# A routed mixture layer on one core: sums of W on ScalarE, scales and split from chunk 3, the last two pieces inside the dense tile, zeros multiplied at the start

## The chip, the core and the metric

The kernel runs on one core of a Trainium2 chip. A core has TensorE (PE, matrix products into the PSUM banks), VectorE (DVE), ScalarE (ACT), GpSimd (POOL) and SyncE (SP, which here only issues transfers). Each engine works through its own list of instructions in order, and engines wait for one another with semaphores. The metric is the device time of one execution in microseconds; lower is better.

## What is computed

The reference in short (x is 8 sequences of 512 tokens of 256 numbers, in float32):

```python
# first half: an attention of which only the row sums are used
q, k = rope((x @ Wq.T).astype(bf16)), rope((x @ Wk.T).astype(bf16))
o = where(causal, exp(q @ k.T / 16), 0).sum(-1)            # one number a token
x = layernorm(x + relu(o @ fc1_w.T + fc1_b) @ fc2_w.T + fc2_b)
# second half: 12 experts, top 3 of three routers over a = x @ P_w.T
C1, C2, C3 = (softmax over the top 3 of a @ U.T, zero elsewhere, for U in (U1, U2, U3))
h = gelu(sum_e C1[:, e] * (x @ W1[e].T))
y = sum_e C2[:, e] * (h @ W2[e].T) + C3 @ b2
out = layernorm(x + y)
```

## The kernel before, in words

The 4096 tokens are 32 tiles of 128, in eight groups of four. A first stage of eight chunks (`NCH` = 8, four sequences by 128 positions each) computes q and k. Per chunk TensorE makes four projections (`project(c, 0..3)`, four float32 matmuls each), ScalarE copies each out of its bank (`qk_copy`, L497), VectorE rotates queries and keys (`rope(c, 0)` and `rope(c, 1)`), TensorE multiplies them (`scores`), ScalarE takes exponentials with their sums (`exps`), and `gate_transpose` with `gate_relu` bring the sums into place for `fc`. A projection uses one of two banks, and `project` waits until the copy of the projection two before it is done.

W1 and W2, 12 experts each, arrive in float32 and are split into a high and a low float16 part after they were multiplied by a power of two found from their largest magnitude. For W1 VectorE takes that maximum (`w_amax`, three reductions, L977); for W2 ScalarE takes the sum of magnitudes as a bound (`w_sum`, three operations, L514), which VectorE reads in `w_bound` (L985). `peak_transpose` (TensorE), `peak_pow` (VectorE), `peak_spread` (TensorE) and `scales` (VectorE, L999 to L1005, ends in `scale_done`) make the factors of all partitions; `router_split` splits the routers' matrix. Eight of the 12 experts of each W are split by GpSimd, one in each `w_piece` (L377, L379, L380; 16 pieces); the other four of each by ScalarE's `w_high` (L532) with VectorE's `w_low` (L1010), 8 pairs. From chunk 4 on there is one piece at each of the 16 places (c, j), j from 0 to 3, and two pairs per chunk.

Between these lie the steps of groups 0 and 1, placed by hand: `early_aux(c, j, early)` calls step 4(c-3)+j of a list of 18, so they begin at place (3, 0), number 12 of 32, and end at place (7, 1), number 29. On GpSimd they are `norm_scale(0)` at place 15, `norm_scale(1)` at 23, `chosen_exps(0)` (L396) at 28 and `weights_of(0)` (L404 to L407) at 29, each ahead of the piece of its place. VectorE waits for `chosen_exps(0)` in `route_sums(0)` (L1090), which stands at place 29 ahead of both rotations of chunk 7. After the chunks VectorE makes the ids of the chosen experts (`route_ids(0)`, L1080 to L1085).

Then comes the dense tile: tile 0 is multiplied by all 12 experts (`first`, `mixture`, L830; a slot is one expert, six matmuls), while the others use the three experts that their group needs. The slots of the dense tile use two banks in turn, so slot n waits until slot n-2 is taken. ScalarE takes slot 0 (`begin(0)`, which waits for the weights of the routers, `C_done`), VectorE adds the others (`first_mixture`, L1188). In TensorE's order `C3_transpose(0)` (L770), which waits for the ids, stands ahead of the first slot. The last scores, gates and the logits of group 1 lie among the slots. The remaining tiles follow, each with a first mixture, a transpose, a second mixture, and a normalisation.

Of the kernel before, what the change touches and what calls it, by code (L numbers as in the profile page):

```python
# [77 lines left out]
def build(nc, x, xT, wqkT, gate, fc2, p_w, uT, w1T, w2T, b2e, constb, constf, out):  # L78
    ctx = ExitStack()
    with ctx:  # L80
# [85 lines left out]
        RING, HT = 4, 4  # L166
        Z = GT * NR * NE
# [121 lines left out]
        def group(g):  # L289
            return 0 <= g < NG  # L290
# [67 lines left out]
        def _(pool):  # L358
# [81 lines left out]
            for c in range(NCH):  # L440
                for j in range(4):
                    early_aux(c, j, early)
                    if c >= 4:
                        w_piece(piece)
                        piece += 1
# [37 lines left out]
        def _(act):  # L483
# [26 lines left out]
            def w_sum(q):  # L510


                act.wait_ge(ld_w[1], 32)
                act.activation(junk[:, :, :], Wf[:, WS:2 * WS, :][:, PARTS[q], :], ACT.Abs,  # L514
                               accum_out=amaxp[:, 1, q:q + 1]).then_inc(asum_done, 1)
                if q < 2:
                    act.wait_ge(asum_done, q + 1)
# [56 lines left out]
            def aux(k, s, pos):  # L574
                if (s, pos) == (0, 0):
                    if group(k + 1):
                        x1_high(k + 1, 1)
                    if group(k):
                        C3T_copy(k)
                if (s, pos) == (1, 0) and group(k + 1):  # L580
                    exp_route(k + 1)
                if (s, pos) == (2, 0) and group(k + 2):
                    normed(k + 2, 0)
                if (s, pos) == (2, 1) and group(k + 2):
                    normed(k + 2, 1)
                if (s, pos) == (3, 0) and group(k + 2):
                    x1_high(k + 2, 0)
# [16 lines left out]
            act.wait_ge(ld_const, 16 * 6)  # L604
            for c in range(NCH):
                qk_copy(c, 0)
                qk_copy(c, 1)
                if c:
                    exps(c - 1, 0)
                early_aux(c, 0, early)  # L610
                early_aux(c, 1, early)
                if c == 2:
                    w_sum(1)
                if c >= 4:
                    w_high(2 * (c - 4))
                qk_copy(c, 2)
                if c:
                    exps(c - 1, 1)
                qk_copy(c, 3)
                if c:  # L620
                    gate_relu(c - 1)
                early_aux(c, 2, early)
                early_aux(c, 3, early)
                if c in (1, 2):
                    w_sum(2 * (c - 1))
                if c >= 4:
                    w_high(2 * (c - 4) + 1)
# [3 lines left out]
            begin(0)  # L631
            exps(NCH - 1, 0)
            exps(NCH - 1, 1)
# [45 lines left out]
        def _(pe):  # L679
# [32 lines left out]
            def peak_transpose():  # L712
                pe.wait_ge(amax_done, 3)
                pe.transpose(bank[MISC][0:3, 0:P], amax[:, :], identf[:, :]).then_inc(peak_done, 1)
# [83 lines left out]
            def aux(k, s, pos):  # L798
                if (s, pos) == (0, 0) and group(k):
                    C3_transpose(k)  # L800
# [49 lines left out]
            pe.wait_ge(ld_const, 16 * 6)  # L850
            pe.wait_ge(ld_qk, 16)
            for c in range(NCH):
# [3 lines left out]
                if c == 0:  # L856
                    for k in range(NC):
# [3 lines left out]
                if c == 3:  # L861
                    peak_transpose()
                early_aux(c, 1, early)
                if c:
                    scores(c - 1, 0)
                project(c, 2)
                early_aux(c, 2, early)
# [3 lines left out]
                if c == 3:  # L871
                    peak_spread()
# [13 lines left out]
            first(range(0, 4))  # L886
            scores(NCH - 1, 0)
# [59 lines left out]
        def _(dve):  # L947
# [26 lines left out]
            def w_amax(q):  # L974
                if q == 0:
                    dve.wait_ge(ld_w[0], 32)
                r = dve.tensor_reduce(amaxp[:, 0, q:q + 1], Wf[:, 0:WS, :][:, PARTS[q], :], AX.XY, ALU.max,  # L977
                                      apply_absolute_value=True)
                if q == 2:
                    link(r)  # L980
                    dve.tensor_reduce(amax[:, 1:2], amaxp[:, 0, :], AX.X, ALU.max).then_inc(amax_done, 1)

            def w_bound():
                dve.wait_ge(asum_done, 3)
                dve.tensor_reduce(amax[:, 2:3], amaxp[:, 1, :], AX.X, ALU.max).then_inc(amax_done, 1)  # L985
# [169 lines left out]
            for c in range(NCH):  # L1155
                early_aux(c, 0, early)
                early_aux(c, 1, early)
                if c == 4:
                    scales()
                    router_split()  # L1160
# [3 lines left out]
                if c == 1:  # L1164
                    w_amax(0)
                if c == 3:
                    peak_pow()
                early_aux(c, 2, early)
                if c >= 4:
                    w_low(2 * (c - 4))  # L1170
                early_aux(c, 3, early)
                rope(c, 1)
                if c == 1:
                    w_amax(1)
                if c == 2:
                    w_amax(2)
                    w_bound()
                if c >= 4:
                    w_low(2 * (c - 4) + 1)
# [11 lines left out]
            def first_mixture(t):  # L1191
# [5 lines left out]
                for j in range(1, experts_of(t)):  # L1197
# [4 lines left out]
                    add_slot(t, 0, j, sums, sums)  # L1202

# [133 lines left out]
```

## Time and profile before

| | |
|---|---|
| median of 3 runs | 327.04 us (326.6 to 327.73) |
| the profiled execution | 327.78 us, span 325.9 us |
| TensorE busy | 284.7 us (87%) |
| VectorE busy | 256.9 us (79%) |
| ScalarE busy | 155.6 us (48%) |
| GpSimd busy | 115.3 us (35%) |
| mean granted TensorE clock | 0.973 |

In 40 equal slices of the span (8.1 us each), busy tenths of each engine and the granted clock of TensorE in tenths, 9 standing for 90% or more:

```profile
PE   0999999979854988999999899899899997999981
DVE  0069789999976479689889979988988987997672
ACT  1137747655661371435635544634743663634231
POOL 1000018999999102141332431332323314133221
PEclk9999999998995999999999999999999999999997
```

The stage of the chunks is in slices 2 to 12; the dense tile is in slices 13 to 15. GpSimd is busy throughout from slice 7 to slice 13, and slices 12 and 13 are those in which TensorE does least after the start.

### The profile page before, as it was taken

Reading aid. Unit: us, or ns where it says so; the run is one execution under the profiler, and the core shown is the slowest. Engines: PE = TensorE matmul, PEld = TensorE weight load, DVE = VectorE, ACT = ScalarE, POOL = GpSimd, SP = SyncE. Lnnn points to the kernel's source line nnn. Section 1 sums busy time; section 2 is a strip of 40 time slices with the busy share of each in tenths; the row PEclk is TensorE's granted clock in tenths of the full one; section 3 lists DMA queues with packets and bytes.
Section 4 is the critical chain, followed back from the end, with each engine's and each line's share of the span. In section 5 each row is a group of like instructions: output and inputs, shape, how many; then the busy total and the mean of one; then the engine's idle time right before and its main releaser. Section 6 shows DMA issues by size and latency. Waiting matters only on the chain.

```text
span 325.9 us, 6342 instructions
## 1 busy us (share of the span) xinstructions
PE 284.7 (87%) x1978; PEld 191.6 (59%) x1978; DVE 256.9 (79%) x849; ACT 155.6 (48%) x327; POOL 115.3 (35%) x264
## 2 busy tenths in 40 slices
PE   0999999979854988999999899899899997999981
PEld 0444455444323667676677577668577566667771
DVE  0069789999976479689889979988988987997672
ACT  1137747655661371435635544634743663634231
POOL 1000018999999102141332431332323314133221
PEclk9999999998995999999999999999999999999997
DMA  8999999700000000000010000000000010010111
GB/s 230 413 411 218 202 187 186 114 2 0 0 1 0 3 2 0 16 20 18 16 35 16 18 16 27 26 18 19 23 27 19 18 32 19 17 34 19 31 33 37
DMA packets 19235, 20.58 MB, mean 63 GB/s; under 512 B 1600, under 2 KB 18432, under 8 KB 18688
## 3 DMA queue, kind: packets, MB, share of 16 engines
q1 hardware_dynamic: 18480, 19.22, 24.2%
q10 hardware_dynamic: 720, 0.93, 1.0%
q8 instruction: 18, 0.29, 0.4%
q14 instruction: 17, 0.14, 0.1%
HBM read 15.94 MB, written 4.19 MB: 62 GB/s over the span
## 4 chain that ended last, share of the span: by engine, by line
PE 35%; DVE 32%; POOL 16%; issue 7%; ACT 6%; DMA 2%; ACTq 0%; DVEq 0%; POOLq 0%
PE bank L830 20%; DVE early L1188 11%; PE bank L686 9%; POOL W L380 5%; POOL wtmp L377 4%; POOL W L379 3%; DVE st L1225 3%; DVE stats L1036 2%; DVE early L1230 2%; POOL rstd L389 2%; DVE top L1057 2%; DMA gatew<-in_gate 2%; ACT x L546 2%; DVE zrest L1068 2%; PE bank L782 2%
## 5 line engine op out<-in xcount | busy, mean ns | idle before, releaser
L830 PE MATMUL bank<-W,early 128*128 (+1 forms) x630 | 75.6, 273 | 6.3 <-DVE early L1188 4.0
L830 PE MATMUL bank<-W,x1T 128*128 (+1 forms) x630 | 77.3, 278 | 0.5 <-DVE early L1188 0.3
L686 PE MATMUL bank<-early,wqk 128*128 128x512 f32 x128 | 65.1, 642 | 8.6 <-DMA gatew<-in_gate 8.6
L830 PEld LDWEIGHTS bank<-W,x1T 128*128 128x128 f16 x630 | 60.5, 99 | 19.9 <-DVE early L1188 9.5
L830 PEld LDWEIGHTS bank<-W,early 128*128 128x128 f16 x630 | 59.5, 98 | 18.2 <-issue 6.0
L1188 DVE SCALAR_TENSOR_TENSOR early<-bank,Csel,early 128x256 f32<-128x256 f32 x124 | 59.4, 479 | 11.6 <-PE bank L830 7.0
L455 POOL TENSOR_SCALAR ve<-mv 128x1 f32<-128x1 f32 x32 | 7.3, 229 | 120.4 <-DVE mv L1226 120.4
L686 PEld LDWEIGHTS bank<-early,wqk 128*128 128x128 f32 x128 | 23.7, 201 | 30.6 <-issue 21.4
L602 ACT ACTIVATE early<-early 128x256 f32<-128x256 f32 x32 | 13.3, 417 | 50.1 <-DVE early L1188 49.9
L497 ACT ACTIVATE qk<-bank 128x512 bf16<-128x512 f32 x32 | 19.0, 594 | 36.7 <-PE bank L686 36.4
L597 ACT ACTIVATE early<-bank,Csel 128x256 f32<-128x256 f32 x31 | 14.6, 472 | 31.0 <-PE bank L830 30.7
L963 DVE TENSOR_TENSOR xcos<-qk,cb 128x1024 bf16<-128x1024 bf16 x16 | 11.8, 740 | 21.1 <-ACT qk L497 21.0
L388 POOL TENSOR_SCALAR ve<-mv 128x4 f32<-128x4 f32 x8 | 2.3, 283 | 65.9 <-DVE mv L1040 65.8
L645 ACT ACTIVATE early<-bank,ipow 128x256 f16<-128x256 f32 x32 | 15.0, 468 | 17.3 <-PE bank L914 17.3
L380 POOL TENSOR_TENSOR W<-wtmp,W 128x512 f16<-128x512 f32 x16 | 21.0, 1316 | 1.4
L655 ACT ACTIVATE early<-early,shift,rstd 128x256 f32<-128x256 f32 x32 | 18.8, 586 | 5.1 <-POOL shift L457 5.1
L1047 DVE TENSOR_TENSOR x1T<-bank,x1T 128x512 f16<-128x512 f32 x16 | 11.0, 688 | 12.3 <-ACT x1T L553 12.3
L546 ACT ACTIVATE x<-xs,shift,rstd 128x256 f32<-128x256 f32 x32 | 17.4, 591 | 4.3 <-POOL shift L391 4.3
L456 POOL TENSOR_TENSOR rstd<-ve,minus_half 128x1 f32<-128x1 f32 x32 | 18.2, 570 | 2.7
L730 PE MATMUL bank<-fc2s,hgT 32*128 32x256 f32 x64 | 18.0, 400 | 0.0
L782 PE MATMUL bank<-b2s,C3T 64*128 64x512 f32 x32 | 18.0, 641 | 0.0
L507 ACT ACTIVATE expd<-bank 128x128 bf16<-128x128 f32 (+3 forms) x32 | 13.7, 437 | 8.8 <-PE bank L701 8.7
(105 smaller groups left out, 434.0 us busy)
## 6 DMA issues: line engine op xcount, KB each, us to landing
early<-in_xT SPq DMA_DIRECT2D x16, 256.0 KB, 9.4
xs<-in_x SPq DMA_DIRECT2D x32, 128.0 KB, 7.2
out<-early SPq DMA_DIRECT2D x32, 128.0 KB
W<-in_w1T SPq DMA_DIRECT2D x1, 2048.0 KB, 12.1
W<-in_w2T SPq DMA_DIRECT2D x1, 2048.0 KB, 12.3
W<-in_w1T SPq DMA_DIRECT2D x1, 1024.0 KB, 7.7
W<-in_w2T SPq DMA_DIRECT2D x1, 1024.0 KB, 13.8
wqk<-in_wqkT ACTq DMA_DIRECT2D x1, 512.0 KB, 3.9
```

The costliest lines, as they stand in the source:

```text
L380: pool.tensor_tensor(W[:, m, e + 1, 1, :], wtmp[:, n % 2, :], W[:, m, e + 1, 0, :], ALU.subtract)\
L456: link(pool.tensor_tensor(rstd2[:, p:p + 1], ve2[:, p:p + 1], minus_half[:, 0:1], ALU.pow))
L497: act.activation(qk[:, c % 2, g, :, :].rearrange("p s n -> p (s n)"), bank[PROJ[n % 2]][:, :], ACT.Copy)\
L546: n = act.activation(x1[:, g % 3, t, :], xs[:, GT * g + t, :], ACT.Identity, bias=shift[:, g % 2, t:t + 1], scale=rstd[:, g % 2, t:t + 1])
L597: act.activation(acc1[:, t % 2, :], bank[place[n]][:, 0:DIM], ACT.Copy, scale=c0).then_inc(acc_begun, 1)
L645: act.activation(hT[:, t % 2, 0, :, :].rearrange("p c n -> p (c n)"), bank[HT][:, 0:DIM], ACT.Copy, scale=ipow2[:, 1:2]).then_inc(hhi_done, 1)
L655: act.activation(y[:, t % 4, :], y[:, t % 4, :], ACT.Identity, bias=shift2[:, p:p + 1], scale=rstd2[:, p:p + 1]).then_inc(y_done, 1)
L686: mm = pe.matmul(bank[PROJ[n % 2]][:, :], wqk[:, k, g, :], xTb[:, c % 4, k, :, :].rearrange("p s n -> p (s n)"), start=(k == 0), stop=(k = ...
L730: mm = pe.matmul(bank[ROWS][:, t % 2 * DIM:(t % 2 + 1) * DIM], hgT[PAD * T:PAD * (T + 1), u, :, :].rearrange("p b r -> p (b r)"), fc2s[PAD ...
L782: mm = pe.matmul(bank[ROWS][:, :], C3T[rows, :], b2s[rows, :], start=True, stop=True)
L830: mm = pe.matmul(where[:, 0:DIM], lhs(hx, c), w, start=(k == 0), stop=(k == 5))
L1188: dve.scalar_tensor_tensor(sums, bank[place[n]][:, 0:DIM], c, before, ALU.mult, ALU.add)\
```

## The change

Five things are moved or replaced.

1. TensorE multiplies 28 times 128 columns of zeros (read from the cleared C3) by 256 columns of zeros before its first projection, and waits for the constants only after `project(0, 1)`. ScalarE's wait for them is moved behind its first two copies.
2. All six sums of |W| run on ScalarE: W1's in chunk 1, W2's in chunk 2, one in the middle and two at the end of each. VectorE's three maxima are gone, and `w_bound` reads all six.
3. `w_bound` is moved behind `rope(3, 0)`, `peak_transpose` behind `scores(2, 0)`, `peak_spread` behind `project(3, 2)`, and the scales with the routers' split from chunk 4 to chunk 3, ahead of `rope(3, 1)`.
4. GpSimd takes its pieces at places 14 to 29 instead of 16 to 31. Of the eight pairs of `w_high` and `w_low` the first comes at the end of chunk 3, two in each of chunks 4 and 5, one in chunk 6, none in chunk 7: the pairs 6 and 7 are moved into the dense tile, `w_low` behind the adds of slots 2 and 6.
5. `C3_transpose(0)` stands behind slot 3 instead of ahead of slot 0, and `C3T_copy(0)` behind `begin(0)`.

```diff
-                    if c >= 4:
+                    if 14 <= 4 * c + j < 30:
                         w_piece(piece)
...
-            act.wait_ge(ld_const, 16 * 6)
             for c in range(NCH):
                 qk_copy(c, 0)
                 qk_copy(c, 1)
+                if c == 0:
+                    act.wait_ge(ld_const, 16 * 6)
...
-                if c == 2:
-                    w_sum(1)
-                if c >= 4:
-                    w_high(2 * (c - 4))
+                if c in (1, 2):
+                    w_sum(c - 1, 0)
+                if 4 <= c < NCH - 1:
+                    w_high(2 * (c - 4) + 1)
...
                 if c in (1, 2):
-                    w_sum(2 * (c - 1))
-                if c >= 4:
-                    w_high(2 * (c - 4) + 1)
+                    w_sum(c - 1, 1)
+                    w_sum(c - 1, 2)
+                if 3 <= c < NCH - 2:
+                    w_high(2 * (c - 3))
...
             begin(0)
+            C3T_copy(0)
+            w_high(NM * NB - 2)
             exps(NCH - 1, 0)
+            w_high(NM * NB - 1)
...
-            pe.wait_ge(ld_const, 16 * 6)
+            pe.wait_ge(zero_done, 4)
+            zeros = C3[:, :, :].rearrange("p t n -> p (t n)").bitcast(BF16)
+            for n in range(WARM):
+                pe.matmul(bank[SCORE[n % 2]][:, 0:DIM], zeros[:, 0:P], zeros[:, :], start=True, stop=True)
...
-                if c == 3:
-                    peak_transpose()
                 early_aux(c, 1, early)
                 if c:
                     scores(c - 1, 0)
+                if c == 3:
+                    peak_transpose()
                 project(c, 2)
+                if c == 3:
+                    peak_spread()
...
             first(range(0, 4))
+            C3_transpose(0)
             scores(NCH - 1, 0)
...
-            def w_amax(q):
...
-                dve.wait_ge(asum_done, 3)
-                dve.tensor_reduce(amax[:, 2:3], amaxp[:, 1, :], AX.X, ALU.max).then_inc(amax_done, 1)
+                dve.wait_ge(asum_done, 3 * NM)
+                dve.tensor_reduce(amax[:, 1:3], amaxp[:, :, :], AX.X, ALU.max).then_inc(amax_done, 1)
...
-                if c == 4:
-                    scales()
-                    router_split()
                 rope(c, 0)
...
-                if c == 1:
-                    w_amax(0)
                 if c == 3:
+                    w_bound()
                     peak_pow()
                 early_aux(c, 2, early)
-                if c >= 4:
-                    w_low(2 * (c - 4))
+                if 4 <= c < NCH - 1:
+                    w_low(2 * (c - 4) + 1)
                 early_aux(c, 3, early)
+                if c == 3:
+                    scales()
+                    router_split()
                 rope(c, 1)
...
+                if 3 <= c < NCH - 2:
+                    w_low(2 * (c - 3))
...
                     add_slot(t, 0, j, sums, sums)
+                    if t == 0 and j in (2, 6):
+                        w_low(NM * NB - 2 + j // 4)
```

## Rows read from the trace of the kernel before

**Rows 1.** Chain that ended last, start: start us, us, what it was.

```profile
2.87 5.70 DMA gatew<-in_gate
8.61 6.65 PE bank L686 x8
...
25.33 1.77 PE bank L686 x4
```

**Rows 2.** The same chain, from chunk 3 to the dense tile.

```profile
38.05 2.30 DVE amaxp L977
...
50.26 0.18 DVE scale L1005
...
50.53 0.77 POOL wtmp L377
...
91.82 0.42 POOL ez L396
...
102.47 4.77 PE bank L830 x24
```

**Rows 3.** Timeline of TensorE: start us, us, instruction, in brackets idle time before.

```profile
71.81 0.77 PE L753 MATMUL bank<-MT,x1T 128*128 128x36 f16 x24 [1.67 <-DVE x1T L1047]
72.42 3.59 PE L686 MATMUL bank<-early,wqk 128*128 128x512 f32 x4
...
87.70 0.60 PE L699 MATMUL bank<-x1T,qr 128*128 128x512 bf16 x2 [0.99 <-DVE x1T L971]
...
94.18 0.22 PE L762 MATMUL bank<-mask,cb 128*1 128x24 bf16 x3
102.02 0.45 PE L770 MATMUL bank<-identf,C 128*128 128x128 f32 x1 [7.62 <-DVE ids L1085]
...
111.16 3.77 PE L830 MATMUL bank<-W,x1T 128*128 128x256 f16 x30
```

**Rows 4.** Timeline of ScalarE in chunk 2, around a sum of W.

```profile
28.30 1.89 ACT L514 ACTIVATE junk<-W 128x2048 bf16<-128x2048 f32 x1
...
30.31 1.30 ACT L497 ACTIVATE qk<-bank 128x512 bf16<-128x512 f32 x2
```

**Rows 5.** Timeline of VectorE from the wait for GpSimd to its first add.

```profile
92.27 0.30 DVE L1090 TENSOR_REDUCE esum<-ez 128x12 f32<-128x144 f32 x1 [1.33 <-POOL ez L396]
...
102.39 0.67 DVE L1047 TENSOR_TENSOR x1T<-bank,x1T 128x512 f16<-128x512 f32 x1
105.53 0.48 DVE L1188 SCALAR_TENSOR_TENSOR early<-bank,C,early 128x256 f32<-128x256 f32 x1 [2.47 <-PE bank L830]
```

**Rows 6.** Timeline of GpSimd: last clearing, a norm between two pieces, last piece.

```profile
1.38 0.20 POOL L370 MEMSET C<- 128x128 f32 x1
...
73.45 0.55 POOL L388 TENSOR_SCALAR ve<-mv 128x4 f32<-128x4 f32 x1
...
75.82 0.70 POOL L377 TENSOR_SCALAR wtmp<-W,scale 128x512 f32<-128x512 f32 x1
...
103.75 0.70 POOL L377 TENSOR_SCALAR wtmp<-W,scale 128x512 f32<-128x512 f32 x1
...
106.30 0.19 POOL L419 COPY Csel<-C 128x3 f32 x1
```

**Rows 7.** Transfers of chunk 0 (issues from 0.7 to 1.3 us), by tile.

```profile
DMA to landing us min/median/max: 4.6/5.3/5.9
```

**Rows 8.** Groups of instructions by line, VectorE: count, busy us, mean ns of one.

```profile
L1010 DVE SCALAR_TENSOR_TENSOR W<-W,scale 128x512 f16<-128x512 f32 x8 | 8.9, 1107 | 0.2
...
L977 DVE TENSOR_REDUCE amaxp<-W 128x1 f32<-128x2048 f32 x3 | 6.9, 2285 | 0.1
```

**Rows 9.** Timeline of VectorE: rotation, statistics and scales in chunk 3, one multiply later.

```profile
41.18 0.69 DVE L963 TENSOR_TENSOR xcos<-qk,cb 128x1024 bf16<-128x1024 bf16 x1
...
43.30 0.28 DVE L990 TENSOR_REDUCE peak<-bank 3x1 f32<-3x128 f32 x1
...
45.06 1.40 DVE L1036 BATCH_NORM_STATS2 stats<-xs 128x6 f32<-128x256 f32 x4
...
49.54 0.16 DVE L999 COPY pow<-bank 128x3 f32<-128x3 f32 x1
...
77.88 1.64 DVE L964 TENSOR_TENSOR xsin<-qk,cb 128x1024 bf16<-128x1024 bf16 x1
```

**Rows 10.** One stretch by engine: busy us (instructions), granted clock, DMA share, GB/s.

```profile
73.00:74.00 1.00, 1.00 (x2) 0.34 (x1) 0.97 (x2) 0.00 (x0) 0.91 (x2) 0.50 0.00 0
```

More of the change, by code:

```diff
@@ L166, in build @@
         RING, HT = 4, 4
+        WARM = 28
         Z = GT * NR * NE
@@ L508, in exps, with w_sum @@
                                    scale=float(DIM) ** -0.5, accum_out=o[:, c % 2, s:s + 1]).then_inc(exp_done, 1)
[L510 to L517, printed above, removed]
+            def w_sum(m, q):
+                act.wait_ge(ld_w[m], 32)
+                wait(act, asum_done, 3 * m + q)
+                act.activation(junk[:, :, :], Wf[:, WS * m:WS * (m + 1), :][:, PARTS[q], :], ACT.Abs,
+                               accum_out=amaxp[:, m, q:q + 1]).then_inc(asum_done, 1)
             def gate_relu(c):
@@ L577, in aux @@
                         x1_high(k + 1, 1)
-                    if group(k):
+                    if group(k) and k > 0:
                         C3T_copy(k)
@@ L712, in peak_transpose @@
             def peak_transpose():
-                pe.wait_ge(amax_done, 3)
+                pe.wait_ge(amax_done, 2)
                 pe.transpose(bank[MISC][0:3, 0:P], amax[:, :], identf[:, :]).then_inc(peak_done, 1)
@@ L798, in aux @@
             def aux(k, s, pos):
-                if (s, pos) == (0, 0) and group(k):
+                if (s, pos) == (0, 0) and group(k) and k > 0:
                     C3_transpose(k)
@@ L856, in _ @@
                 if c == 0:
+                    pe.wait_ge(ld_const, 16 * 6)
                     for k in range(NC):
@@ L870, in _ @@
                 project(c, 3)
-                if c == 3:
-                    peak_spread()
                 early_aux(c, 3, early)
@@ L972, in rope @@
                 dve.wait_ge(rope_done, 2 * c + part + 1)
-            def w_amax(q):
[L975 to L981, printed above, removed]
             def w_bound():
-                dve.wait_ge(asum_done, 3)
-                dve.tensor_reduce(amax[:, 2:3], amaxp[:, 1, :], AX.X, ALU.max).then_inc(amax_done, 1)
+                dve.wait_ge(asum_done, 3 * NM)
+                dve.tensor_reduce(amax[:, 1:3], amaxp[:, :, :], AX.X, ALU.max).then_inc(amax_done, 1)
             def peak_pow():
@@ L1163, in _ @@
                     router_matrix()
-                if c == 1:
-                    w_amax(0)
                 if c == 3:
+                    w_bound()
                     peak_pow()
                 early_aux(c, 2, early)
-                if c >= 4:
-                    w_low(2 * (c - 4))
+                if 4 <= c < NCH - 1:
+                    w_low(2 * (c - 4) + 1)
                 early_aux(c, 3, early)
+                if c == 3:
+                    scales()
+                    router_split()
                 rope(c, 1)
[L1173 to L1179, printed above, removed]
+                if 3 <= c < NCH - 2:
+                    w_low(2 * (c - 3))
             route_ids(0)
```

## The prediction

> **What bounds the kernel now.** I read the chain of work that ended last first, in order of time, because the change touches only the first 117 us of a span of 325.9 us; what follows is the same code. The chain there has four links. Until 8.61 us TensorE waits for the last constant. Its first eight projection matmuls then take 6.65 us, where later ones take 1.77 us for four: two projections that cost 3.54 us at the full rate cost 3.1 us more [rows 1]. From there TensorE is the bound through chunks 1, 2 and 3, with one hop over VectorE's last maximum of |W| at 38.05. At 50.43 the scales are there, and the chain passes to GpSimd, which splits W piece after piece without a pause until `chosen_exps(0)`, 91.82 to 92.24, the operation that VectorE waits for [rows 2]. The last link is VectorE: sums, two rotations, two `w_low`, the ids at 101.9; TensorE has stood still since 94.4, and the dense tile begins at 102.0, at half rate [rows 2, 3]. ScalarE is not on this chain: its sums of W take 2.0 us each from start to the start of what follows, and nobody waits for them [rows 4].
>
> So the number to follow is when GpSimd reaches `chosen_exps(0)`: VectorE stands 1.33 us in front of its result [rows 5], TensorE waits for VectorE, and no later stage makes up for it.
>
> **The start.** `zero_done` is complete when the memset of C3 ends, at 1.6 us [rows 6]. The 28 products of zeros have 256 columns each. In the dense tile 24 such products took 4.77 us at the half rate, 0.2 us each [rows 2], so 28 take at most 5.7 us and end at 7.4, or sooner if the clock rises among them. Chunk 0 is in 5.9 us after its second issue at 1.3, at 7.2 [rows 7]. I take 7.4 for the first projection, at the full rate: 1.2 us from the earlier start and 3.05 us from the rate, 4.25 us together (4.45 at best; 1.0 if zeros do not lift the clock, which no row shows). Moving the wait for the constants behind `project(0, 1)` costs nothing: they are there at 8.6 [rows 1], and that point is now reached at 10.9. ScalarE's same move is covered likewise, and VectorE's wait for them is as before. The end of `project(1, 3)`, which I call t, moves from 27.10 [rows 1] to 22.85.
>
> **ScalarE's sums.** Six instead of three, and VectorE is rid of three maxima of 2.29 us [rows 8]. But VectorE was not the bound there beyond the one hop, and TensorE can run only two projections ahead of ScalarE's copies, since these have two banks. After `project(1, 3)`: copy and ReLU to t+1.2, two sums to t+5.3, the copy of (2, 0) to t+5.9 [rows 4]. TensorE has done (2, 0), (2, 1) and two scores by t+4.4 and stands for 1.5 us. The sum in the middle of chunk 2 is just covered, and the two at its end reach t+15.4, as `project(3, 1)`, with `fc(0, 0)` before it, ends at t+15.25.
>
> **The order in chunk 3.** `w_bound` now stands behind `rope(3, 0)` on VectorE. That rotation needs the copy of (3, 1), t+16.5, and takes 2.1 us [rows 9]; the bound ends at t+18.8. `peak_transpose` stands on TensorE behind `scores(2, 0)`, which are done at t+15.7. TensorE waits for 3.2 us, with `project(3, 2)`, `fc(0, 1)` and all of chunk 4 queued behind. Then 0.3 us for the transpose, 1.77 for `project(3, 2)` (`peak_pow` is hidden under it), 0.3 for the spread, 1.05 for `fc(0, 1)`: t+22.4. VectorE adds it (0.7) and takes the statistics of group 0 (1.8 us), then come the scales, 0.95 us [rows 9]: t+25.85, against t+23.3 before. On top comes the clock. A stall of 1.67 us before 71.8 was followed by a granted clock of 0.50, and four projection matmuls took 3.59 us instead of 1.77; a stall of 0.99 us before 87.7 was not [rows 3, 10]. 3.2 us is nearly twice the former, so I add 1.8 us once; for the 1.5 us of chunk 2 I take nothing (1.8 more at worst). Scales: 22.85 + 25.85 + 1.8 = 50.5, against 50.43. The whole gain of the start is used up here. The bounds are 46.2 (t+23.3, no stall) and 52.3.
>
> **The queue on GpSimd.** Pieces are taken at places 14 to 29 instead of 16 to 31. `norm_scale(0)` (about 2.2 us) was done before the first piece and now stands behind it; `chosen_exps(0)` stands at place 28, behind 14 pieces instead of 12. Twelve pieces with one `norm_scale` took 50.53 to 91.82, 41.3 us [rows 2]; less 2.4 us for the norm [rows 6] that is 3.24 us a piece. Now 14 x 3.24 = 45.4, 2.2 + 2.4 for two norms, 0.5 for `chosen_exps`, 0.1: 50.5 us from the scales to its end, where it was 41.8. The distance grows by 8.7 us, and the scales come no sooner. A piece beside an idle VectorE took 2.55 us (103.75 to 106.30) [rows 6]; as VectorE will idle before the result, I take off 1.2 us for the last two. `chosen_exps(0)` ends at 50.5 + 50.5 - 1.2 = 99.8, 7.6 us later than at 92.24. Behind that wait are queued on VectorE `route_sums`, both rotations of chunk 7, `route_ids(0)` and the whole dense tile.
>
> **Behind it.** From 92.24 to 103.06, where VectorE was ready for its adds [rows 5], are 10.8 us; two `w_low` leave it, 1.11 us each [rows 8]: 8.65 us. VectorE is ready at 108.45. Before, its first add ran only at 105.53 [rows 5], since TensorE began with `C3_transpose` behind the ids and then at half rate [rows 3]. Now TensorE has slots 0 and 1 done long before, slot 2 as soon as ScalarE begins the tile, and only slot 3 waits for an add: 2.5 us back. From the first add to the end of slot 11 were 105.53 to 114.93, 9.4 us [rows 3, 5]. Into this stretch come two `w_low`, the first behind slot 3, `C3_transpose`, `C3T_copy` and `w_high(6)`. VectorE idles between its adds, which covers half: 10.5 us (9.4 if all is covered; 12.5 if nothing is and slot 3's chain comes on top). Slot 11 ends at 108.45 + 10.5 = 118.95, against 114.93. ScalarE's two `w_high` lie beside VectorE's adds.
>
> **The sum.** Start -4.25, stalls and order in chunks 2 and 3 +2.55, clock +1.8, queue +8.7, its shorter last pieces -1.2, `w_low` out of the tail -2.2, no wait behind the ids -2.5, `w_low` and its waits in the tile +1.1: +4.0. The profiled execution took 327.78 us around its span of 325.9, and this makes it 331.8. The median of the runs lies 0.74 below the profiled one: **331.0 us**, 1.2% slower.
>
> **The rivals.**
> - The clock holds through the stall of 3.2 us: 1.8 us less, 329.2. For it: a stall of 0.99 us did no harm. Against: one of 1.67 us did [rows 3, 10].
> - ScalarE's sums and the new order hold TensorE up nowhere. The scales come at 46.2, and the rest of the sum gives 331.0 - 1.8 - 2.5 = 326.7: no change. For it: three sums so far passed without a stall [rows 4]. Against: two projections ahead is all that two banks allow, and two sums now stand in a row twice.
> - Faster: the pieces shrink. VectorE's second multiply of a rotation takes 1.64 us beside pieces, while the whole rotation took 2.1 before them [rows 9]. If GpSimd is slowed by VectorE as much, a VectorE with less to do lets a piece fall to 2.55 us. It decides from 2.95 us a piece on (4.0 us over 14 pieces). At 2.55 GpSimd would have the result before VectorE comes for it, at about 93: 6.7 us less than 99.8, 324.3. Against: until 91 us VectorE has the same rotations and still six `w_low` to do. The Trainium skill (SBUF — State Buffer, "Who interferes with whom") has it that a VectorE instruction with two SBUF inputs contends with a GpSimd instruction that reads SBUF, and that the one issued second blocks until the first ends. By that rule pieces beside the rotations stay as long as they are; the trace agrees, with 2.55 us beside an idle VectorE and 3.24 us on the mean [rows 2, 6].
> - The zeros don't lift the clock. Only 1.0 us of the start is gained, 3.2 us less: 334.2. The Trainium skill (TensorE: Matmul & The Clock Gate, "What's actually happening") says that the gate goes by how busy the array is, which would count zeros like other data; no row here shows it.
>
> **How the numbers follow.** Forecast 0.50; the clock holds 0.19; no hold-up 0.12; pieces shrink 0.13; zeros in vain 0.06. A measurement of this kernel can tell about 0.3%, 1 us, from no change. So faster 0.13, same 0.12, slower 0.75. The range runs from 326.7, which takes in the case of no change, to 333.5, the forecast with 1.8 us for the clock in chunk 2 and 0.7 for waits in the tile; the fast case and the vain zeros are left out.
>
> **What would show it.** A first projection near 7.4 us at the full rate. A gap of some 3 us on TensorE before the peak transpose and a granted clock of 0.50 behind it. `scale_done` near 50. Fourteen pieces before `ez`, which ends near 100, and VectorE idle for 6 us before it. It is wrong if the scales come at 46 or sooner, or if pieces take less than 3 us on the mean.

## The result and the profile after

The changed kernel takes 331.77 us (median of 4 executions, 330.87 to 332.72), the kernel before 326.82 beside it: a ratio of 1.0151 (95% interval 1.0104 to 1.0198). 331.0 us were forecast. Its profiled execution took 330.93 us with a span of 328.9, 3.15 us above the profiled one of before, where the sum says +4.0.

The slices of the page, 8.2 us each, of TensorE, GpSimd and the granted clock:

```profile
PE   7998697979792998999899999899999997998981
...
POOL 1000019999998002131431432332324223123221
PEclk9999999997996799999999999999999999999998
```

TensorE works from the first slice on now, but slice 13 holds a 2, and GpSimd's block of work ends in the same slice as before, the thirteenth. The chain that ended last (start us, us, what), in the stretch that [rows 1, 2] show of before:

```profile
1.26 5.99 DMA early<-in_xT
...
7.39 3.67 PE bank L691 x8
...
24.11 2.00 ACT junk L516 x2
...
28.72 1.98 PE bank L691 x4
...
41.22 0.17 DVE amax L987
41.43 0.27 PE bank L719
...
47.88 0.18 DVE scale L1007
48.11 0.14 issue
48.24 0.71 POOL wtmp L378
...
51.41 0.57 POOL ve L389
...
97.22 0.43 POOL ez L397
...
106.78 0.40 DVE early L1184
...
114.39 3.61 PE bank L835 x30
```

Read against [rows 1, 2]: the first eight projection matmuls take 3.67 us instead of 6.65 and start 1.2 us sooner. ScalarE's sums (`junk`) have come onto the chain, where none stood. The scales are there at 48.05 instead of 50.43, `chosen_exps(0)` (`ez`) ends at 97.64 instead of 92.24, and slot 11 at 118.0 instead of 114.93. The end of `project(1, 3)` moved from 27.1 to 22.9. So 4.2 us were won by then, 1.8 us of them were lost by the scales, and GpSimd's stretch from the scales to `ez` grew from 41.8 to 49.6 us. The tail behind it, `ez` to slot 11, shrank from 22.7 to 20.4. -2.4 + 7.8 - 2.3 = +3.1 us, the difference of the two executions (3.15 us) to a tenth.

TensorE and VectorE in the changed kernel (start us, us, instruction, in brackets idle time before and what ended it), beside [rows 3, 5]:

```profile
1.63 5.26 PE L859 MATMUL bank<-C 128*128 128x256 bf16 x28 [1.63 <-POOL C L371]
...
28.72 1.98 PE L691 MATMUL bank<-early,wqk 128*128 128x512 f32 x4 [1.56 <-ACT qk L498]
...
41.43 0.27 PE L719 MATMUL bank<-identf,amax 128*3 128x128 f32 x1 [2.94 <-DVE amax L987]
...
103.00 1.46 PE L835 MATMUL bank<-W,x1T 128*128 128x256 f16 x6 [3.62 <-ACT early L597]
107.23 1.46 PE L835 MATMUL bank<-W,x1T 128*128 128x256 f16 x6 [2.77 <-DVE early L1184]
```

```profile
97.67 0.30 DVE L1092 TENSOR_REDUCE esum<-ez 128x12 f32<-128x144 f32 x1 [3.17 <-POOL ez L397]
...
106.71 0.98 DVE L1184 SCALAR_TENSOR_TENSOR early<-bank,C,early 128x256 f32<-128x256 f32 x2
109.86 0.75 DVE L1012 SCALAR_TENSOR_TENSOR W<-W,scale 128x512 f16<-128x512 f32 x1 [2.17 <-ACT W L532]
```

Both stalls of TensorE before the scales are there, 1.56 and 2.94 us. Before the dense tile's third and fourth slot it stands again, for ScalarE and then for VectorE. Both of these had stood for GpSimd: VectorE was idle for 3.17 us in front of `ez`, where it was 1.33 us before [rows 5], and ScalarE began the tile when GpSimd's weights of the routers were there:

```profile
102.47 0.47 ACT L597 ACTIVATE early<-bank,C 128x256 f32<-128x256 f32 x1 [3.48 <-POOL C L408]
```

### The profile page after: what moved, and what is told of

It reads as the page before. It is cut to its first block, busy times and chain, and to the rows that moved or that the text cites. A ratio compares the mean times of both kernels' runs of the same rounds, so it can differ in the third digit from the quotient of the medians.

```text
span 328.9 us, 6402 instructions
## 1 busy us (share of the span) xinstructions
PE 287.4 (87%) x2004; PEld 194.5 (59%) x2006; DVE 249.3 (76%) x845; ACT 161.0 (49%) x333; POOL 114.0 (35%) x264
## 4 chain that ended last, share of the span: by engine, by line
PE 31%; DVE 31%; POOL 18%; issue 8%; ACT 8%; DMA 2%; DVEq 0%; SPq 0%; POOLq 0%; ACTq 0%
PE bank L835 19%; DVE early L1184 11%; PE bank L691 6%; POOL W L381 5%; POOL wtmp L378 4%; POOL W L380 3%; DVE stats L1038 3%; DVE st L1223 3%; DVE early L1228 2%; POOL rstd L390 2%; DMA early<-in_xT 2%; DVE top L1059 2%; ACT x L546 2%; DVE zrest L1070 2%; PE bank L787 2%
## 5 line engine op out<-in xcount | busy, mean ns | idle before, releaser
L691 PE MATMUL bank<-early,wqk 128*128 128x512 f32 x128 | 61.8, 614 | 2.1 <-ACT qk L498 1.6
L691 PEld LDWEIGHTS bank<-early,wqk 128*128 128x128 f32 x128 | 22.8, 194 | 22.9 <-issue 20.1
L378 POOL TENSOR_SCALAR wtmp<-W,scale 128x512 f32<-128x512 f32 x16 | 15.5, 970 | 46.7 <-DVE scale L1007 46.7
L381 POOL TENSOR_TENSOR W<-wtmp,W 128x512 f16<-128x512 f32 x16 | 20.4, 1276 | 1.4
L1184 DVE SCALAR_TENSOR_TENSOR early<-bank,Csel,xs 128x256 f32<-128x256 f32 x31 | 14.8, 478 | 2.6 <-PE bank L835 2.4
## 6 DMA issues: line engine op xcount, KB each, us to landing
W<-in_w2T SPq DMA_DIRECT2D x1, 2048.0 KB, 12.3
W<-in_w2T SPq DMA_DIRECT2D x1, 1024.0 KB, 13.8
```

The costliest lines, as they stand in the source:

```text
L378: link(pool.tensor_scalar(wtmp[:, n % 2, :], Wf[:, WS * m + e + 2, :], scale[:, 1 + m:2 + m], 0.0, ALU.mult, ALU.add))
L381: pool.tensor_tensor(W[:, m, e + 1, 1, :], wtmp[:, n % 2, :], W[:, m, e + 1, 0, :], ALU.subtract)\
L691: mm = pe.matmul(bank[PROJ[n % 2]][:, :], wqk[:, k, g, :], xTb[:, c % 4, k, :, :].rearrange("p s n -> p (s n)"), start=(k == 0), stop=(k = ...
L1184: dve.scalar_tensor_tensor(sums, bank[place[n]][:, 0:DIM], c, before, ALU.mult, ALU.add)\
```

## The experiments

Each was timed beside the kernel before on the same chip. They ran in three rounds: the start alone, the queue, the order in chunk 3 and the changed kernel again; then the tile, the exchanged weights and the two kernels built on them; then the last three. The kernel before had a median of 326.75, 326.56 and 326.74 us in them. The diffs show the lines that matter; where one of them builds on an earlier kernel, the text says on which.

**The start alone.** The kernel before with this:

```diff
+            pe.wait_ge(zero_done, 4)
+            zeros = C3[:, :, :].rearrange("p t n -> p (t n)").bitcast(BF16)
+            for n in range(WARM):
+                pe.matmul(bank[SCORE[n % 2]][:, 0:DIM], zeros[:, 0:P], zeros[:, :], start=True, stop=True)
-            pe.wait_ge(ld_const, 16 * 6)
...
+                if c == 0:
+                    pe.wait_ge(ld_const, 16 * 6)
```

> The kernel before with the start of the changed one alone: 28 products of zeros, TensorE's wait for the constants behind project(0, 1), ScalarE's behind its first two copies. My theory: the start is worth 4.2 us by itself and nothing takes it back, since the sums, the scales and the queue on GpSimd keep their order. The end of project(1, 3) at 22.9 us, the scales at 46.2, GpSimd's chosen_exps(0) done near 88.1, the time 4.2 us below the kernel before (ratio 0.987). Rival: the later links (VectorE before chosen_exps, transfers that land no sooner) hold what comes after chunk 3, and less than 2 us arrive at the end.

Measured: 325.12 us, ratio 0.9957 (0.9942 to 0.9972), 1.6 us below the kernel before. My expectation of 4.2 failed. ScalarE and TensorE in this kernel:

```profile
26.20 1.91 ACT L515 ACTIVATE junk<-W 128x2048 bf16<-128x2048 f32 x1 [2.12 <-DMA W<-in_w2T]
```

```profile
28.89 2.85 PE L688 MATMUL bank<-early,wqk 128*128 128x512 f32 x4 [1.88 <-ACT qk L498]
```

The early start runs into a transfer. The order of the kernel before sums W2 first on ScalarE, and W2's last part lands at 26.2 us. The transfers of W2 are issued at 7.4 and 13.9 us in both kernels and take as long (12.3 and 13.8 to 13.9 us), so they land no sooner. Two copies stand behind that sum, and TensorE behind the copies. In this profile the clock fell behind the stall as well, and the scales came only at 49.90; at 326.80 us it is the slowest of the seven executions. The rival had the size right (less than 2 us arrive) and named transfers, but put the loss behind chunk 3; it begins in chunk 1. The changed kernel sums W1 in chunk 1, which is there at 17, and so it needs its new order to keep what the zeros give. My prediction counted that order only as a cost.

**The queue on GpSimd.** The changed kernel with:

```diff
-                    if 14 <= 4 * c + j < 30:
+                    if c >= 4:
```

> The changed kernel with GpSimd's pieces back at places 16 to 31, all else as changed: norm_scale(0) ahead of the first piece and 12 pieces ahead of chosen_exps(0). My theory (the queue on GpSimd is the largest loss): the scales stay at 48.0, chosen_exps(0) is done near 91 instead of 97.6, but VectorE comes for it only at 94.5, where the profile of the changed kernel has it idle for 3.2 us, so the time falls by 3.2 us against the changed kernel and is about that of the kernel before. Rival: the pieces' number ahead does not matter, as the stalls in chunks 2 and 3 made everything late: no difference to the changed kernel.

Measured: 325.99 us, ratio 0.9968 (0.9945 to 0.9991), where the changed kernel beside it had 332.24: 6.2 us less, twice what I expected, and 0.8 us below the kernel before. The rival, no difference, falls. This kernel's profile is its slowest execution, 328.77 us, with the clock down in chunk 3: the scales come at 50.49 and `ez` ends at 95.08. The same kernel ran once more, and one in between, with the pieces at places 15 to 30:

> The changed kernel with the pieces back at places 16 to 31, once more, since its profile fell into an execution in which the clock dropped in chunk 3 (scales at 50.5 us). My theory: the median is again 5 to 6 us below the changed kernel's, and in an execution with the scales near 48 chosen_exps(0) is done near 92.5, 5 us before the changed kernel's 97.6, with VectorE's arrival moved too. Rival: the first result was the spread of the runs, and only 3 to 4 us remain, as between the two profiles that both show the drop.

> The changed kernel with the pieces at places 15 to 30: norm_scale(0) ahead of the first piece and 13 pieces ahead of chosen_exps(0) instead of 14. My theory: the end goes with the queue ahead of chosen_exps as long as VectorE is idle there (3.2 us with 14 ahead), so one piece less gives 3.0 us against the changed kernel and leaves VectorE almost without idle time. Rival: with 12 ahead the gain was 5.8 us because norm_scale(0) behind the first piece had made group 0's own chain late; then this kernel, which has the norm ahead too, gains most of it, 5 us.

Measured: 326.62 us, ratio 0.9983 (0.9953 to 1.0014), with 12 pieces ahead, and 328.45 us, 1.0043 (1.0021 to 1.0066), with 13; the changed kernel, with 14, stands at 1.0151 and 1.0177. VectorE before `ez` in the second profile with 12 ahead, with 13, and in a profile of the changed kernel with its scales as late as theirs (50.0, 49.6 and 49.8 us):

```profile
93.92 0.30 DVE L1092 TENSOR_REDUCE esum<-ez 128x12 f32<-128x144 f32 x1 [0.15 <-POOL ez L397]
```

```profile
96.46 0.30 DVE L1092 TENSOR_REDUCE esum<-ez 128x12 f32<-128x144 f32 x1 [3.40 <-POOL ez L397]
```

```profile
99.39 0.30 DVE L1092 TENSOR_REDUCE esum<-ez 128x12 f32<-128x144 f32 x1 [3.16 <-POOL ez L397]
```

`ez` ends at 99.4, 96.4 and 93.9 us: each piece ahead of `chosen_exps(0)` costs 2.5 to 2.9 us, nearly its length. The end follows. The single executions of each of these kernels fall into two groups: about 330.9 and 332.6 us with 14 ahead, 327.7 and 329.3 with 13, 325.0 and 326.7 with 12 (and two executions near 329). Group by group the steps are 3.2 and 2.7 us. The medians say 3.3 to 3.8 and 1.8 us, because they fall now into the lower group and now into the upper. The expectation for 13 ahead was 3.0 us. For the repeat with 12 ahead it was 5 to 6 us, and 5.2 to 5.6 came, so its rival of 3 to 4 us falls.

I had taken VectorE's arrival, 94.5 us in the changed kernel, as a floor. It is none: with 13 ahead VectorE is there at 93.06 although the scales are 1.5 us later than in that profile, and idle as long as with 14, where I had expected almost no idle time. From the scales to the arrival it is 46.5 us in both profiles with 14 ahead and 43.5 to 43.8 with 13 and with 12, so one step moved it and the next did not. Two things differ between 14 and 13 ahead. `norm_scale(0)` comes behind or ahead of the first piece; and `norm_scale(1)` ends late enough with 14 that TensorE waits for group 1's normalised tokens (here in the second profile of the changed kernel), which it does in none of the other three:

```profile
85.84 0.66 PE L744 MATMUL bank<-identf,x 128*128 128x128 f32 x4 [1.44 <-ACT x L546]
```

No run separates the two. The rival, that the norm's place gives most of 5 us, falls: 13 ahead gives 3.5 to 4.4 us by the ratios, and 12 ahead a further 1.8 or more.

**The order in chunk 3.** The changed kernel with `w_bound` and `peak_pow` ahead of the rotation:

```diff
+                if c == 3:
+                    w_bound()
+                    peak_pow()
                 rope(c, 0)
...
-                if c == 3:
-                    w_bound()
-                    peak_pow()
```

> The changed kernel with w_bound and peak_pow ahead of rope(3, 0) on VectorE, all else as changed. My theory: TensorE's stall of 2.94 us before the peak transpose goes, since the last sum of W is there at 38.1 us and VectorE is free then; the scales come 2.8 us sooner (45.3), GpSimd starts and ends its 14 pieces 2.8 us sooner, and so does the end: 2.8 us below the changed kernel. Rival: the rotation that now comes 1.4 us later holds scores(3, 0) and the copies, and half of it or more is lost again.

Measured: 328.24 us, ratio 1.0051 (1.0031 to 1.0071), 4.0 us below the changed kernel beside it. VectorE in this kernel:

```profile
45.07 0.17 DVE L1007 TENSOR_SCALAR scale<-ipow 128x3 f32<-128x3 f32 x1
...
94.86 0.30 DVE L1092 TENSOR_REDUCE esum<-ez 128x12 f32<-128x144 f32 x1 [1.48 <-POOL ez L397]
```

The scales come 2.81 us sooner than in the changed kernel and `ez` 2.8 us sooner, to the tenth as expected; the rival's loss did not show. The median fell by more than that. The changed kernel beside it was in its upper group with all four executions; against the lower group, 330.9 us, the median is 2.7 us less. The profiles differ by 3.6 us, 2.8 of them up to the first add and 0.7 between there and slot 11, where the half clock covers less of the stretch (until about 107 us, 3.4 behind the first add, against 111.6 and 4.9).

**The changed kernel again.**

> The changed kernel itself once more, because its four times lie in two pairs, 330.9 and 332.7 us, 1.8 us apart, which is what one fall of the granted clock to 0.50 for about 3.5 us costs. My theory: the times fall into the same two groups again, and a profile from the upper one shows the half clock after the stall of 2.9 us in chunk 3, where the first profile kept 1.00. Rival: the difference comes from elsewhere (transfers at the start), and the projections behind that stall take 1.77 us in each profile.

Measured: 332.24 us, ratio 1.0177 (1.0147 to 1.0207), single executions from 331.98 to 333.09, none near 330.9 this time, so the two groups came again only in part. The profile is of 332.5 us. TensorE behind the peak transpose in it:

```profile
41.50 0.38 PE L719 MATMUL bank<-identf,amax 128*3 128x128 f32 x1 [2.94 <-DVE amax L987]
41.67 3.47 PE L691 MATMUL bank<-early,wqk 128*128 128x512 f32 x4
```

And 41 to 45 us by engine, here and in the first profile, busy us with counts, then the granted clock, DMA share and GB/s:

```profile
41.00:45.00 4.00, 3.50 (x5) 1.17 (x5) 1.19 (x6) 0.00 (x0) 0.00 (x0) 0.57 1.15 165
```

```profile
41.00:45.00 4.00, 3.57 (x15) 1.92 (x16) 1.38 (x7) 0.60 (x1) 0.00 (x0) 1.00 1.14 168
```

The stall is 2.94 us in both. In one the clock goes to half and `project(3, 2)` takes 3.47 us, in the other it stays and the projection takes 1.88 us. The scales follow: 49.77 against 48.05. The 1.7 us are there at slot 11 (119.6 against 118.0) and at the end (332.5 against 330.9). So the same stall costs a half clock in some executions and not in others. The rival, that the difference comes from elsewhere and the projection takes 1.77 us in each profile, falls. In the profile of the kernel without the stall there is no such fall before the scales. That fits with the 4.0 us that its removal gave by the medians of this round, against 2.8 by the scales, but one profile does not show that the fall never comes there.

**The dense tile alone.** The kernel before with the moved `C3_transpose(0)`, its copy and the last two pairs:

```diff
             first(range(0, 4))
+            C3_transpose(0)
...
             begin(0)
+            C3T_copy(0)
+            w_high(NM * NB - 2)
             exps(NCH - 1, 0)
+            w_high(NM * NB - 1)
...
-                if c >= 4:
+                if 4 <= c < NCH - 1:
...
+                    if t == 0 and j in (2, 6):
+                        w_low(NM * NB - 2 + j // 4)
```

> The kernel before with one part of the change alone: pairs 6 and 7 of w_high and w_low and C3_transpose(0) with its copy inside the dense tile; start, sums, scales and the places of the pieces as before. My theory: this part is a gain by itself. From the end of chosen_exps(0) at 92.2 us VectorE is ready for its adds 8.7 us later, at 100.9, and from there the changed kernel needs 11.3 us to the end of slot 11: 112.2 instead of 114.9, 2.7 us below the kernel before. Rival: the waits that come into the tile (w_low behind w_high, behind the copy of C3, behind the transpose) cost what the shorter tail gives: no difference.

Measured: 324.38 us, ratio 0.9934 (0.9912 to 0.9957), 2.2 us below the kernel before, where 2.7 were expected. The rival of no gain falls. From the end of `ez` to the end of slot 11 its profile has 20.2 us, 2.5 less than before. Two rows of its TensorE:

```profile
8.72 5.17 PE L689 MATMUL bank<-early,wqk 128*128 128x512 f32 x8 [8.72 <-DMA gatew<-in_gate]
...
107.28 3.77 PE L833 MATMUL bank<-W,x1T 128*128 128x256 f16 x30
```

The second ends the dense tile, at 111.05. The first shows something else: the first eight projection matmuls, with nothing on TensorE ahead of them, are the same in this kernel as before and took 5.17 us here and 6.65 in [rows 1]. The price of the cold start is itself 1.6 to 3.1 us from one execution to the next. With zeros ahead they took 3.67 us in all eleven profiles of kernels that have them.

**The start with the weights exchanged.** The kernel with the start alone, with `peak_transpose` and the three maxima moved as the expectation says, and:

```diff
-                act.wait_ge(ld_w[1], 32)
-                act.activation(junk[:, :, :], Wf[:, WS:2 * WS, :][:, PARTS[q], :], ACT.Abs,
+                act.wait_ge(ld_w[0], 32)
+                act.activation(junk[:, :, :], Wf[:, 0:WS, :][:, PARTS[q], :], ACT.Abs,
...
-                    dve.wait_ge(ld_w[0], 32)
+                    dve.wait_ge(ld_w[1], 32)
```

> The kernel before with the start of the changed one, and with the two weights exchanged: ScalarE takes its three sums of W1 at the same places, VectorE its three maxima of W2, one behind rope(1, 1), rope(2, 0) and rope(2, 1) each; peak_transpose stands behind scores(2, 0). My theory: in the kernel with the zeros alone ScalarE stood 2.1 us before its first sum until the last transfer of W2 landed at 26.2, with two copies behind it, and this swallowed the start's gain. W1 is there at 17, so that wait goes; VectorE's last maximum ends near 37.5 and holds the peak transpose by about 1.2 us. The time is 3 us below the kernel before. Rival: the gain of the start is lost later whatever waits for W2, and the time stays at that of the zeros alone, 1.5 us below the kernel before.

Measured: 323.75 us, ratio 0.9910 (0.9892 to 0.9928), 2.8 us below the kernel before and 1.4 below the start alone. TensorE waits 0.55 us for the peak instead of the 1.2 expected:

```profile
37.80 0.27 PE L716 MATMUL bank<-identf,amax 128*3 128x128 f32 x1 [0.55 <-DVE amax L991]
```

Its first sum starts at 24.49 without a wait, and TensorE's stall of 1.88 us is gone, so the wait for W2 was one part of the loss, and the rival falls. It is about half: of the 2.6 us that were missing, 1.2 to 1.5 came back. The rest, 1.1 to 1.4 us, is not accounted for. The cold start of the executions before varies by as much, and the maxima on VectorE now hold TensorE for 0.55 us.

**Both parts, and one piece moved.** The two kernels above in one; then, on top, the piece of place 27 behind the last:

```diff
-                    if c >= 4:
+                    if c >= 4 and 4 * c + j != 27:
                         w_piece(piece)
                         piece += 1
+            w_piece(piece)
             select_of(0)
```

> The two kernels above in one: start, exchanged weights, and the last two pairs with C3_transpose(0) inside the dense tile; GpSimd's pieces at places 16 to 31. My theory: the parts lie in different stretches of one chain, so their gains add: 5.7 us below the kernel before. Rival: the shorter tail meets another bound (VectorE at the wait for chosen_exps, the pieces of W2 at the second mixture), and less than 4 us arrive.

> As the kernel with both parts, and GpSimd's piece of place 27 put behind the last one, so that 11 pieces instead of 12 stand ahead of chosen_exps(0). My theory (the number of pieces ahead of chosen_exps sets the end as long as VectorE is idle before it): VectorE was idle there for 1.2 to 1.3 us in the kernels with 12 ahead and for 3.2 us with 14, so one piece less gives 1.2 us and no more, where a piece lasts 3.2 us. Rival: VectorE arrives later than thought, and nothing is gained.

Measured: 321.94 us, ratio 0.9847 (0.9826 to 0.9868), and 319.89 us, 0.9812 (0.9775 to 0.9849). The first is 4.6 us below the kernel before, where 5.7 were expected; its parts gave 2.8 and 2.2, so they add within 0.4 us, and the rival, less than 4 us, falls. The second takes 2.05 us more off, where I had 1.2; its rival, no gain, falls. VectorE in the first and GpSimd in the second:

```profile
88.64 0.30 DVE L1100 TENSOR_REDUCE esum<-ez 128x12 f32<-128x144 f32 x1 [1.33 <-POOL ez L397]
```

```profile
85.82 0.46 POOL L397 TENSOR_TENSOR ez<-ez,mask 128x144 f32<-128x144 f32 x1 [0.91 <-DVE mask L1086]
```

With 11 ahead GpSimd waits for VectorE's mask, no longer VectorE for GpSimd. The 1.33 us of VectorE's wait are the 1.2 expected. The two profiles are 2.56 us apart, and 2.05 us of that are already there at the first add (97.69 against 95.64): VectorE goes on from `ez` 1.5 us sooner, and its way from there to the first add is 0.5 us shorter. The last 0.5 us come in the dense tile, and there the clock differs. It fell to 0.50 ahead of slot 3 in both, at 96.7 and at 95.8 us, but from 100 to 104 us it was granted 0.56 in the first and 1.00 in the second:

```profile
100.00:104.00 4.00, 4.00 (x20) 2.42 (x19) 2.31 (x3) 2.79 (x7) 2.86 (x8) 0.56 0.00 0
```

```profile
100.00:104.00 4.00, 3.53 (x30) 2.64 (x29) 2.83 (x7) 2.24 (x7) 3.78 (x9) 1.00 0.00 0
```

TensorE stood for 1.8 and 3.4 us ahead of slots 2 and 3 in the first, for 3.2 us ahead of slot 3 in the second; that this made the half clock longer is not shown. The second is the fastest kernel of the study, 1.9% below the kernel before by the ratio and 3.6% below the changed one.

**The changed kernel mended.** Its own sums, with the order in chunk 3 and the places of the last two experiments.

> The changed kernel with its two orders mended: w_bound and peak_pow ahead of rope(3, 0), pieces at places 16 to 31 with that of place 27 behind the last, so that 11 stand ahead of chosen_exps(0); all six sums stay on ScalarE. My theory: what the change does otherwise is a gain, and the scales come at 45.3 us against 46.7 in the kernel with ScalarE summing W1 alone; VectorE then sets the end, and it comes out within 1 us of that kernel (319.9). Rival: the sums on ScalarE cost more than VectorE's maxima did, through TensorE's stall of 1.6 us in chunk 2 and the clock, and it lies 2 us above.

Measured: 321.63 us, ratio 0.9819 (0.9779 to 0.9859), 1.7 us above the best by the medians of two rounds, the same within the intervals by ratio. This does not tell the two theories apart. Its VectorE, and TensorE in chunk 7:

```profile
45.19 0.17 DVE L1008 TENSOR_SCALAR scale<-ipow 128x3 f32<-128x3 f32 x1
...
93.26 1.33 DVE L975 TENSOR_TENSOR xcos<-qk,cb 128x1024 bf16<-128x1024 bf16 x1 [1.69 <-ACT qk L499]
```

```profile
85.38 0.38 PE L705 MATMUL bank<-x1T,qr 128*128 128x512 bf16 x1 [2.35 <-DVE x1T L983]
...
86.14 3.63 PE L692 MATMUL bank<-early,wqk 128*128 128x512 f32 x4
```

The scales come at 45.36 as expected, and GpSimd is out of the way, but now VectorE waits for a copy in chunk 7. The rows show why. TensorE stood for 2.35 us for VectorE's rotation, the clock fell behind that (0.56 from 86 to 88 us), the next projection took 3.63 us, and its copy was late for VectorE. So this profile, 322.46 us, has a fall of the clock on its chain; two of the four executions took 320.6 and 320.8 us, and no profile shows whether it is absent there. What is shown is that the change's parts are worth 1.8% together once two orders in it are put right.

## Why the prediction was right, step by step

The steps as forecast, in the first profile of the changed kernel, and in the second, where the clock fell:

| step | forecast | first | second |
|---|---|---|---|
| first projection, us | 7.4 | 7.39 | 7.46 |
| stall in chunk 2 | 1.5 | 1.56 | 1.56 |
| stall before the peak | 3.2 | 2.94 | 2.94 |
| scales there | 50.5 (48.7 if the clock holds) | 48.05 | 49.77 |
| `chosen_exps(0)` done | 99.8 | 97.64 | 99.36 |
| VectorE idle before it | 6 | 3.17 | 3.16 |
| first add | 108.45 | 106.71 | 108.42 |
| slot 11 done | 118.95 | 118.0 | 119.6 |
| time of the execution | 331.8 | 330.93 | 332.5 |

- **The start** came as worked out, to a tenth of a microsecond, but its bound for the zeros was a little low. The 24 products in 4.77 us of [rows 2] were not all at half rate (the granted clock rises before they end, 0.63 from 106 to 107 us), and 24 in 4.77 make 5.6 us for 28, not 5.7. The zeros took 5.26 us in the first profile and 5.99 in the second, where the first projection came straight behind them at 7.46. The 3.05 us for the rate come from one execution; as the experiment with the dense tile showed, the cold start costs 1.6 to 3.1 us.
- **The clock** was the one term with two outcomes, and both occurred. The forecast gave the fall 0.50 and the case in which the clock holds 0.19; the first execution is that case. Only two executions were profiled. By their times, six of the eight of the changed kernel lie with the second profile and two with the first.
- **The queue** was the term that decided, and it was right: the stretch from the scales to `ez` is 49.6 us, against 49.3 by the sum (50.5 less 1.2). A piece took 3.1 us on the mean, and the last two 2.6 us each, as the sum had them. The 14 pieces were a little shorter than forecast (43.4 us without the norms, against 44.2) and the two norms longer (5.5 us against 4.6). Taking two pieces out from ahead of `chosen_exps(0)` took 5.2 to 6.2 us off the median.
- **VectorE's arrival** at the wait was off: at 94.5 instead of 93 at the latest. It cost nothing here, since GpSimd was later still, but it made me expect only 3.2 us from the second experiment. With one piece less ahead it came 3.0 us sooner after the scales.
- **The sums on ScalarE** were taken as a cost of 1.5 us. That was measured (1.56), but the start alone showed the other half of the term: with W2 summed first the zeros would have met the transfer of W2. The forecast has no such term because it kept the whole gain of the start in every case. That includes the rival without a hold-up, 326.7 us, a kernel that no run has.
- **The tile** was sized at 9.07 us from `ez` to the first add (forecast 8.65) and 11.3 us from there to slot 11 (forecast 10.5), with VectorE idle for 2.17 us before the first `w_low` as its order said. The sum has this part as a gain of 3.6 us (-2.2, -2.5, +1.1); alone it measured 2.2. In the changed kernel's own profiles this part gave 2.3 and 2.4 us. The term in the tile was too small, 1.9 instead of 1.1 us, and 0.4 us more were lost ahead of the first add. In the profile with `w_bound` ahead of the rotation this stretch took 10.6 us with the same code, and the half clock covered less of it.
- **What luck there was.** In the second profile, which has the fall that was forecast, the scales were 0.7 us early, the stretch to `ez` 0.3 us long and the tail 1.1 us long; they sum to the 0.7 us by which 332.5 lies above 331.8. And the median was put 0.74 us below the profiled execution, while it lies 0.84 us above the first one. That 331.0 came within 0.8 us of 331.77 owes something to errors that cancel. The mechanism, two more pieces ahead of `chosen_exps(0)`, was tested by itself and holds.
- **The rivals.** Pieces did not shrink to 2.95 us on the mean (3.1), so the fast case falls. The zeros did lift the clock: eight matmuls took 3.67 us behind them, against 6.65 and 5.17 without. Only the durations show it, for the granted clock reads 1.00 during the slow ones as well. This is the kernel before, with three matmuls in 2 us:

```profile
10.00:12.00 2.00, 2.00 (x3) 0.67 (x2) 0.00 (x0) 0.00 (x0) 0.00 (x0) 1.00 1.08 451
```

The Trainium skill (TensorE: Matmul & The Clock Gate, "What's actually happening") says that the gate goes by how busy the array has recently been. That zeros count as work is what the case adds, and the durations agree with it.

## What to carry to other kernels

Follow one engine's queue to the operation that others wait for, and count what stands ahead of it: two pieces of W more ahead of a half-microsecond operation that VectorE needed cost this kernel 5 to 6 us, though GpSimd had no more to do than before. A step that starts sooner is worth only what the next transfer and the next queue allow, so test such a gain by itself before the rest is built on it. Where a stall of 2 to 3 us stands before dense matmul work, take the same kernel's profile more than once: whether the clock falls was not the same in each execution here. And compare the single times: when they fall into groups, two medians can differ because one lies in the upper group.

## What had not been expected of the hardware

- The same stall of 2.94 us was followed by a half clock in one execution and by the full one in another, 1.6 us on one projection (3.47 against 1.88), and 1.7 us on all that came after. A shorter one, 1.88 us in the kernel with the start alone, was followed by a fall; 1.56 us in the changed kernel was not, in either profile.
- In chunk 6 of the same two profiles it is the other way round. A stall of 2.19 us at 74.14 was followed by a granted clock of 0.52 (74 to 76 us) in the first, and one of 2.18 us at 75.86 by 1.00 (76 to 78 us) in the second. It did not show in the time: the stretch from the scales to `ez`, in which GpSimd is the bound, is 49.6 us in both.
- The first eight matmuls after 8.6 to 8.7 us without work took 6.65 us in one execution and 5.17 in another, with the same code ahead of them, and the granted clock in the rows is 1.00 in both.
